# Row normalisation of four groups on ScalarE instead of VectorE in a two-layer attention and expert kernel, with layer 1's key weights prepared later

## What is computed

```python
x = x + _L0_xattn_ref(_layernorm(x), ctx_1024, ctx_1024, w_q, w_kv, w_concat)
x = x + _L0_ffn_ref(_layernorm(x), router_w, gate_w, up_w, down_w)
x = x + _L1_xattn_ref(_layernorm(x), ctx_1024, ctx_1024, Wq, bq, Wk, bk, Wv, bv)
x = x + _L1_ffn_ref(_layernorm(x), gate_w, w1, w2, w3, w1s, w2s, w3s)
```

## Time and profile before

| what | before |
|---|---|
| median of three runs | 759.71 us |
| the three runs | 758.55, 759.71, 762.72 us |
| the profiled execution, time | 757.46 us |
| its span, first to last instruction | 755.7 us |
| mean granted clock of TensorE | 0.985 of full |
| busy: PE / DVE / ACT / POOL | 701.6 / 574.0 / 484.5 / 331.8 us |
| first attention's blocks | about 20 to 144 us |
| stores to xn_d, 512 KB, issue to landing | 3.3 us (median of 8) |

### The profile page before, as it was taken

The page is one execution under the profiler, slowest core; times in us unless marked ns, Lnnn a source line. Parts: engine busy times, 40 slices in busy tenths (PEclk is TensorE's granted clock), DMA queues, the critical chain, the costliest instruction groups (busy, mean ns, idle before and its releaser), DMA issues.

```text
span 755.7 us, 14185 instructions
## 1 busy us (share of the span) xinstructions
PE 701.6 (93%) x4989; PEld 622.0 (82%) x4989; DVE 574.0 (76%) x1008; ACT 484.5 (64%) x831; POOL 331.8 (44%) x325
## 2 busy tenths in 40 slices
PE   6899998899999999999999999999899889999994
PEld 6776775678899988999989998999787468898873
DVE  6787777587878778867868786868688867877847
ACT  3477566445567677767767775867567946777740
POOL 6568668402241344135322433232235665777530
PEclk9999999999999999999999999999999899999997
DMA  5000021168568768886867786867470644454438
GB/s 192 1 2 1 1 84 45 51 216 282 172 211 241 264 182 263 253 263 195 264 201 254 238 280 190 253 225 220 112 284 34 222 119 121 143 159 152 131 111 281
DMA packets 58247, 130.63 MB, mean 173 GB/s; under 512 B 6689, under 2 KB 30242, under 8 KB 58178
## 3 DMA queue, kind: packets, MB, share of 16 engines
q1 hardware_dynamic: 46658, 109.09, 41.9%
q0 software_dynamic: 11232, 20.46, 12.2%
q10 hardware_dynamic: 288, 0.19, 0.1%
HBM read 106.90 MB, written 22.81 MB: 172 GB/s over the span
## 4 chain that ended last, share of the span: by engine, by line
PE 64%; DVE 19%; ACT 7%; issue 4%; DMA 3%; POOL 1%; ACTq 1%; DVEq 0%; POOLq 0%; SPq 0%
PE ps L358 56%; DVE w_lo L1353 6%; ACT w_hi L884 2%; PE ps L2482 2%; DVE h_lo L1353 1%; DVE gu L1353 1%; ACT gu L884 1%; DVE hf L2021 1%; PE ps L2439 1%; DVE hf L1796 1%; PE ps L2191 1%; DMA xnb<-y_d 1%; DMA xm_d<-xnb 1%; DVE top_t L1447 1%; ACTq L1271 1%
## 5 line engine op out<-in xcount | busy, mean ns | idle before, releaser
L1353 DVE TENSOR_TENSOR w_lo<-wr,w_hi 128x1024 fp32r<-128x1024 f32 x144 | 175.2, 1222 | 29.0 <-ACT w_hi L884 28.4
L777 POOL DMA_INDIRECT x_d<-ye,sca x39 | 74.5, 1909 | 245.3 <-ACT ye L1060 209.4
L884 ACT ACTIVATE w_hi<-wr 128x1024 fp32r<-128x1024 f32 x144 | 150.7, 1051 | 0.9 <-DMA wr<-in_w 0.9
L358 PE MATMUL ps<-xe_hi,w_hi 128*128 128x256 f32 x480 | 137.4, 286 | 2.0 <-DVE hf L1796 1.8
L358 PE MATMUL ps<-xe_hi,w_lo 128*128 128x256 f32 x488 | 137.8, 283 | 0.0
L358 PE MATMUL ps<-xe_lo,w_hi 128*128 128x256 f32 x480 | 135.8, 283 | 0.0
L358 PEld LDWEIGHTS ps<-xe_hi,w_hi 128*128 128x128 f32 x480 | 92.0, 192 | 5.1 <-DVE xe_lo L1353 3.0
L358 PEld LDWEIGHTS ps<-xe_hi,w_lo 128*128 128x128 f32 x488 | 93.6, 192 | 0.1
L358 PE MATMUL ps<-w_hi,h_hi 128*128 128x256 f32 x312 | 90.9, 291 | 2.6 <-DVE h_lo L1353 2.2
L358 PEld LDWEIGHTS ps<-xe_lo,w_hi 128*128 128x128 f32 x480 | 92.1, 192 | 0.0
L358 PE MATMUL ps<-w_lo,h_hi 128*128 128x256 f32 x312 | 88.2, 283 | 0.0
(11 more groups left out here) (384 smaller groups left out, 1756.9 us busy)
## 6 DMA issues: line engine op xcount, KB each, us to landing
wr<-in_w SPq DMA_DIRECT2D x144, 512.0 KB, 4.8
dr<-in_w1d SPq DMA_DIRECT2D x24, 256.0 KB, 2.7
xn_d<-xnb SPq DMA_DIRECT2D x8, 512.0 KB, 3.3
raw<-in_w1gu SPq DMA_DIRECT2D x8, 512.0 KB, 8.8
x_d<-x_all SPq DMA_DIRECT2D x4, 512.0 KB, 5.5
x_all<-x_d SPq DMA_DIRECT2D x4, 512.0 KB, 4.3
xm_d<-xnb SPq DMA_DIRECT2D x4, 512.0 KB, 4.3
xnb<-y_d SPq DMA_DIRECT2D x4, 512.0 KB, 6.0
```

The source lines that it names most:

```text
L358: return nc.tensor.matmul(out, w, x, start=start, stop=stop, skip_group_check=True)
L777: pool.indirect_dma_start(dst, bass.IndirectOffsetOnAxis(ap=sca[n][:, col + half:col + half + 1], axis=0), ye[:, t % 2, half, :], None, co ...
L884: return s.activation(o, i, ACT.Copy)
L1353: return v.tensor_tensor(o, a, b, ALU.subtract)
```

## The change

ScalarE does the four normalisations, in two pieces of two tiles each, behind the exponentials of steps 8 and 10 (`rows_normed`). VectorE writes the shifts, 128x4 numbers, in a tile of its own `nm_r` (`shift_rows`), at step 8 of g = 0 and 1 and at step 5 of g = 2 and 3. The semaphore `nm0_ok` now counts these four and the one it counted before. Layer 1's key weights stand three blocks later, b = NBLK - 3, step 8 of g = 3.

```diff
@@ ScalarE
+            def rows_normed(g, part):
+                n, k = (na, g + 2) if g < 2 else (nb, g - 2)
+                if part == 0:
+                    act.wait_ge(nm0_ok, g + 1)
+                    if g < 2:
+                        act.wait_ge(na["mm"], KC * (g + 2))
+                    elif g == 3:
+                        act.wait_ge(xn_st, 32)
+                for j in (2 * part, 2 * part + 1):
+                    ins = s.activation(n["x"][:, j, :], x_all[:, k * GT + j, :], ACT.Identity, bias=nm_r[:, g, j:j + 1],
+                                       scale=n["rs"][:, k % 2, j:j + 1])
+                if part:
+                    ins.then_inc(n["xn"], 1)
...
                     s.activation(p_hi[0:w, b % 4, :], ps[0:w, b % 2, :], ACT.Exp, scale=DH ** -0.5).then_inc(p_ex, 1)
+                if st in (8, 10) and g < NG:
+                    rows_normed(g, (st - 8) // 2)
...
             exponents(r0, 1)
-            act.wait_ge(nm0_ok, 1)
+            act.wait_ge(nm0_ok, NG + 1)
@@ VectorE
+            def shift_rows(g, n, k):
+                dve.wait_ge(n["rstd"], k + 1)
+                v.scalar_tensor_tensor(nm_r[:, g, :], n["mv"][:, :, 0], -1.0, n["rs"][:, k % 2, :], ALU.mult, ALU.mult
+                                       ).then_inc(nm0_ok, 1)
...
-                if st == 8 and g + 2 < NG:
-                    dve.wait_ge(na["mm"], KC * (g + 2))
-                    normalise(na, g + 2, tile_of(g + 2))
+                if st == 8 and g < 2:
+                    shift_rows(g, na, g + 2)
...
-                if st == 5 and 2 <= g < NG or st == 4 and g == NG:
-                    if g >= 3:
-                        dve.wait_ge(xn_st, 32 * (g - 2))
+                if st == 5 and 2 <= g < NG:
+                    shift_rows(g, nb, g - 2)
+                if st == 4 and g == NG:
+                    dve.wait_ge(xn_st, 32 * (g - 2))
                     normalise(nb, g - 2, tile_of(g - 2))
...
-                if b == NBLK - 6:
+                if b == NBLK - 3:
                     for e in range(KC):
                         v.tensor_scalar(w1qT[:, e, :], w1qT[:, e, :], wq_mean[:, e:e + 1], D ** -0.5, ALU.subtract, ALU.mult)
```

More of the change, by code:

```diff
@@ L164, in build_program @@
         nm1 = sb("nm1", [P, NG, GT])
+        nm_r = sb("nm_r", [P, NG, GT])
         mx = sb("mx", [P, NT])
```

## The result

| | before | after |
|---|---|---|
| median, us | 759.45 | 755.5 |
| lowest to highest, us (runs) | 756.43 to 762.72 (11) | 753.87 to 757.37 (11) |
| ratio after / before | | 0.9946, 95% interval 0.9929 to 0.9962 |
| profiled execution: span, time, us | 755.7, 757.46 | 755.4, 757.17 |
| mean granted clock in the profiled execution | 0.985 | 0.985 |

The change made the kernel 0.5% faster, 3.95 us by the medians; 754.5 was forecast, a gain of about 5.

The account below looks back on a forecast made before the run. TensorE was taken to bound the stage from 20 to 144 us, so only its pauses and slowed clock could be won. Terms -4.2 + 0.2 (group 3), -1.46 (group 1), +0.3 (group 0) gave -5.2: 754.5 us, range 751.8 to 758.6.

Parts of the forecast that it names:

- The pause before block 41 goes: Group 3 of the first attention: TensorE's wait for VectorE's q_hi, 128.28 to 131.59, disappears; -3.31 us.
- The clock stays up: Behind that group 3 pause, 3.40 us at the lower clock become 1.73; -1.67 us.
- The widening is late next, 0.8 us: Group 3: TensorE next waits 0.8 us for GpSimd's widening of the reciprocals, which ends at 130.54.
- The key weights cost nothing behind: Group 3: the four moved key-weight instructions and product a end by 136.1, before TensorE asks near 136.7; cost 0.
- their far bound: The key weights' four instructions beside GpSimd's gapless run: anything up to 5.7 us, against 1.1 alone.
- g = 1, -1.46: Group 1: q_lo comes once ScalarE has q_hi, near 74.5, so TensorE's wait at the first concat goes; -1.46 us.
- ScalarE's pieces: Eight pieces of two 128x256 activations between ScalarE's exponentials, 1.07 us each, 8.6 in all, without a table load.
- g = 0, +0.3: Group 0: loses the 0.38 us won and 0.3 more, as the piece behind step 10 delays the next exponential; +0.3 net.
- so I expect it to slip through: Group 0, at 44.22: the two-tensor shift is not held beside GpSimd's one-input copy, which lasts until 44.60.
- The rival of the held shift: Shift held at group 0 until 45.9: group 0 costs 1.6, group 1 wins 0.1; -2.5, 757.2 us; chance 0.13.
- forecast and held shift: Two cases set as alternatives: the sum as forecast, 754.5 us, chance 0.50; the shift held, 757.2 us, chance 0.13.
- The forecast of the shift's length, 0.15 us: Each of the four 128x4 shifts on VectorE takes 0.15 us, as such an instruction does elsewhere.

Follow-up runs that it names:

- e_before_again: The kernel before, unchanged, measured again against itself; 760.29 us, ratio 1.0011.
- e_act_extra: The kernel before with eight idle 128x256 activations added on ScalarE where the changed kernel has its pieces, VectorE untouched; 759.99 us, ratio 1.0015.
- e_pause_back: The changed kernel with five unread VectorE reductions put ahead of q_hi of block 41; 759.23 us, ratio 0.9999.
- e_keys_only: The kernel before with only layer 1's key weights moved three blocks later, normalisation left on VectorE; 756.44 us, ratio 0.9951.
- e_after_again: The changed kernel, unchanged, measured again on the chip of the third group; 754.78 us, ratio 0.9937.
- e_g0_single: e_shift_single with the first group's rows left on VectorE as in the kernel before; 751.49 us, ratio 0.9890.
- e_shift_single: The changed kernel with each 128x4 shift written as four VectorE operations on 128x1; 752.91 us in four runs, ratio 0.9911.
- e_single_again: e_shift_single, unchanged, measured again beside e_after_again; 752.52 us, ratio 0.9896.

## Why the prediction was right, and where it was off

**The pause before block 41 goes: right.** 3.31 us became 0.44, and 0 with the unheld shift. VectorE's lateness was the cause: each half of the change shortened the pause, and five idle reductions on VectorE brought it back.

**The clock stays up: right, and the largest risk taken.** Of fourteen traces in this study, the four with a pause of 3.3 to 3.4 us before block 41 (before, e_before_again, e_act_extra, e_pause_back) all have a low stretch there, within 130 to 139 us; the ten with 1.75 us or less have none there. Three of those ten (e_keys_only, e_after_again, e_g0_single) have one from 147.8 to 149.6 us on instead, behind a pause of 1.67 us that stands there before and after the change (TensorE waits for a_lo), and the others go through that pause without. So with 3.3 us the clock fell in all four traces, with 1.7 sometimes. The means over runs carry the same sign: 0.9857 to 0.9869 in the kernels with the long pause, 0.9882 to 0.9908 in the others. One stretch of 3.4 us at half speed is 0.00225 of the mean over 756 us, and costs 1.7 us, so the change of the means, about 0.002, bears out a term near the 1.67 of the prediction. A single execution can differ: 1.3 us in e_pause_back, and in e_before_again 1 us more than in the profile before.

**The widening is late next, 0.8 us: right**, seen whole in e_shift_single. With the held shift it was hidden behind the 0.44 us before the scores.

**The key weights cost nothing behind: right**, though the four took 5.8 us, just past their far bound.

**g = 1, -1.46: right in kind**, -1.3, since the shift was held 1.09 us there; unheld, the stretch won 1.7.

**ScalarE's pieces:** the prediction read that the added function runs between exponentials without a table load. The row that it rests on stands behind an exponential and ahead of a table load (161.32 us), but the reading came true: the changed kernel's trace has no table load between 3 and 160 us.

**g = 0, +0.3: the term that was mis-sized.** It came out as +0.20 where the opening runs late, and as +1.66 in three of the five traces that have the 128x4 shift at g = 0. Of the 1.66, the pieces on ScalarE are 0.5 (30.74 to 30.80 with a shift that is not held, where before has 30.24) and the hold is 1.1. The step that failed is "so I expect it to slip through". The rival of the held shift had this place, this end (its 45.9 became 46.4) and this price (1.6), but what it took from g = 1 (all but 0.1) did not follow: the hold there was 1.09 us, and 1.3 of the 1.46 us came. With +1.66 for +0.2 the sum is -5.06 + 1.46 = -3.6 us, and 759.45 less 3.6 is 755.9, beside 755.5 and 754.8 measured. So forecast and held shift, which I had set against each other as 0.50 and 0.13, both happened: everything forecast was won, and the hold took back 1.1 us at g = 0, in three of five traces, and 0.4 at g = 1, in all. The total still lay within 1 us of the median because the rival that happened beside the forecast cost less than the 2.7 us at which I had priced it, which is luck. How often the hold at g = 0 occurs over all runs is open.

The forecast of the shift's length, 0.15 us, came true once in four (g = 2, 0.16). The rows read for it decided too little: the VectorE product beside GpSimd's normalisation showed that one partner does not hold it, and the place had other partners, a copy and a subtraction. The Trainium skill, "SBUF — State Buffer", section "SBUF: two separate sides", had the rule that applied: it names the VectorE operation with two SBUF inputs and any GpSimd operation that reads SBUF. The traces agree with it four times (0.53, 1.09, 1.69, 3.92 us), and not at 588.64. Nor does a wait for one whole instruction give the 3.92, which ran over three of GpSimd's.

## What to carry to other kernels

An operation of 0.15 us can cost 3.9 where it stands beside another engine's run, and it does not matter how small it is; before an engine's work is replaced by such an operation on the head of somebody's wait, look at what its neighbour does at that moment, and write it in a form that is not held (here four of 128x1, which beat one of 128x4 by 2.3 us, of which the traces place 1.5). A term read from one execution holds for that execution's opening: check a small term at the other time offsets that the opening can give. And a pause that VectorE causes is worth more than its length where TensorE's clock falls behind it.

## What the runs showed of the hardware

- A VectorE scalar_tensor_tensor of 128x4 on two SBUF tensors was held for as long as GpSimd ran two-input subtractions one behind the other: it started at 127.28 beside an iota, and ended with the third subtraction behind it, 3.92 us later. It was not let in between them, which I had not expected; at g = 0 of the first profile it was let in between a subtraction and a copy (0.53 us), and at g = 1 it was not (1.09 us, from the middle of a subtraction to the end of the copy behind it). At g = 2 it took 0.16 us beside an iota, which reads nothing.
- A tensor_scalar of 128x1, its scalars taken from SBUF, was never held: 44 of them in three traces (e_shift_single, e_single_again, e_g0_single) took 202 to 215 ns. The tensor_scalar of 128x256 is held (4.20 us beside a run, 0.34 alone), with one tensor input as well. The Trainium skill, "SBUF — State Buffer", section "SBUF: two separate sides", puts this down to whether the operation runs in a mode that uses both ports; that a 128x1 does not is only what the durations suggest.
- A broadcast copy on VectorE, 128x128, took 1.31 us beside such a subtraction, and 0.21 alone.
- Reductions on VectorE were not held: five of 128x512 took 669 to 673 ns each, 3.04 us together, and GpSimd's subtraction of 129.09 to 130.35 stood beside some of them.
